# Attention with value products in four query quarters, and six key tiles' exponentials summed on GpSimd

## What is computed

```python
def layer(x):
    h = layernorm(x, eps=1e-6)
    q, k, v = split_heads(h @ w_qkv + b_qkv)              # 12 heads, 1024 x 32 each
    attn = (q * scale) @ k.T + rel_h + rel_w              # 1024 x 1024 per head, position terms from q
    x = x + (softmax(attn) @ v).merge_heads() @ w_proj + b_proj
    t = layernorm(x, eps=1e-5)
    # eight groups of 128 tokens, 8 experts, top 2, at most 40 tokens of a group per expert
    x = x + combine(relu(dispatch(t) @ wi[e]) @ wo[e])
    return x
```

## Time and profile before

| | before |
|---|---|
| median of 3 runs | 675.04 us |
| span of the profiled execution, first to last instruction | 670.8 us |
| of the run outside that span (675.04 less 670.8) | 4.2 us |
| PE busy in the span | 639.2 us, 95% |
| DVE, ACT, POOL busy | 391.9, 302.1, 29.4 us |
| share of the chain that ended last on PE | 90% |
| attention, from the first matmul of head 0 to the end of the last values | 81.91 to 333.04 us |

### The profile page before, as it was taken

One profiled execution on the slowest core, in us unless ns is written; L12 is line 12 of the kernel. 1 busy time (PEld: TensorE's weight loads), 2 busy tenths in 40 slices (PEclk: granted clock), 3 DMA queues, 4 the chain that ended last, 5 costly groups with the idle time before them and its releaser, 6 DMA issues.

```text
span 670.8 us, 10479 instructions
## 1 busy us (share of the span) xinstructions
PE 639.2 (95%) x3801; PEld 490.9 (73%) x3801; DVE 391.9 (58%) x664; ACT 302.1 (45%) x419; POOL 29.4 (4%) x49
## 2 busy tenths in 40 slices
PE   2999999999999999999986799999999999999996
PEld 2876845444444455544485699999999999999995
DVE  7557556545654556553176988555755566556735
ACT  4554234443444434444445453445444554444523
POOL 2300000000000000000030000000000000000000
PEclk9999999999999999999996799999999999999999
DMA  8045053331233213310115053445244434444302
GB/s 253 2 86 112 9 111 78 79 71 28 60 78 78 59 27 72 78 35 1 59 37 177 0 179 109 140 155 171 97 142 142 150 131 141 141 141 142 107 0 95
DMA packets 37406, 63.28 MB, mean 94 GB/s; under 512 B 3864, under 2 KB 32894, under 8 KB 37246
## 3 DMA queue, kind: packets, MB, share of 16 engines
q1 hardware_dynamic: 37374, 62.83, 33.6%
HBM read 44.16 MB, written 1.57 MB: 68 GB/s over the span
## 4 chain that ended last, share of the span: by engine, by line
PE 90%; DVE 4%; ACT 3%; DMA 1%; issue 1%; SPq 1%; DVEq 0%
PE ps L692 19%; PE ps L708 19%; PE ps L548 14%; PE ps L538 14%; PE ps L524 8%; PE ps L448 7%; PE ps L663 1%; PE ps L478 1%; PE ps L718 1%; DMA onehot<-c_onehot 1%; DVE rhalf L1034 1%; PE ps L642 1%; PE ps L725 1%; PE ps L555 1%; PE ps L726 1%
## 5 line engine op out<-in xcount | busy, mean ns | idle before, releaser
L1034 DVE TENSOR_REDUCE rhalf<-ps 128x1 f32<-128x512 f32 x192 | 126.7, 687 | 91.1 <-PE ps L524 87.8
L841 ACT ACTIVATE prob<-ps 128x1024 f32<-128x1024 f32 x96 | 98.2, 1023 | 154.6 <-PE ps L538 154.6
L538 PE MATMUL ps<-qst,kst 128*128 128x512 f32 x384 | 107.3, 401 | 0.0
L548 PE MATMUL ps<-prob,vh 128*64 128x512 f32 x384 | 103.6, 618 | 0.1
L692 PE MATMUL ps<-xeh,wih 128*128 128x320 f32 (+1 forms) x288 | 89.7, 312 | 1.0 <-ACT xeh L889 1.0
L538 PEld LDWEIGHTS ps<-qst,kst 128*128 128x128 f32 x384 | 69.9, 188 | 27.9 <-issue 14.6
L708 PE MATMUL ps<-hh,woh 128*128 128x320 f32 x288 | 89.3, 310 | 0.0
L708 PE MATMUL ps<-hl,woh 128*128 128x320 f32 x288 | 89.0, 309 | 0.0
L692 PE MATMUL ps<-xel,wih 128*128 128x320 f32 (+1 forms) x288 | 89.0, 309 | 0.0
L692 PE MATMUL ps<-xeh,wil 128*128 128x320 f32 (+1 forms) x288 | 89.0, 309 | 0.0
L708 PE MATMUL ps<-hh,wol 128*128 128x320 f32 x288 | 89.0, 309 | 0.0
(11 more groups left out here) (153 smaller groups left out, 766.5 us busy)
## 6 DMA issues: line engine op xcount, KB each, us to landing
raw_i<-in_L_ffn_wi SPq DMA_DIRECT2D x32, 576.0 KB, 5.0
raw_o<-in_L_ffn_wo SPq DMA_DIRECT2D x32, 576.0 KB, 4.0
xs<-in_x SPq DMA_DIRECT2D x8, 384.0 KB, 4.6
qst<-qh SPq DMA_DIRECT2D x12, 256.0 KB, 3.1
qst<-relh SPq DMA_DIRECT2D x12, 256.0 KB, 3.9
qst<-relw SPq DMA_DIRECT2D x12, 256.0 KB, 4.5
kst<-kp SPq DMA_DIRECT2D x12, 256.0 KB, 5.2
qst<-ql SPq DMA_DIRECT2D x12, 128.0 KB, 3.1
```

Of the source, the lines that this page charges most:

```text
L538: last = mm(bank(2 * (t % 2) + half), kst[b][:, part, t * P:(t + 1) * P], qst[b][:, part, half * BANK:(half + 1) * BANK], start=part == 0, ...
L548: last = mm(bank(6)[2 * HD * half:2 * HD * (half + 1), :], vh[b][:, t, :], prob[:, t % 2, half * BANK:(half + 1) * BANK], start=t == 0, st ...
L841: run(prob[:, t % 2, :], ps[:, 2 * (t % 2) * BANK:2 * (t % 2 + 1) * BANK], ACT.Exp).then_inc(exp_done, 1)
L1034: ve.tensor_reduce(rhalf[:, p // 2, p % 2:p % 2 + 1], bank(4 + p % 2), AX_X, ALU.max).then_inc(max_red, 1)
```

## The change

The change rebuilds `head` around pairs of key tiles, and does these things:

- **Quarters.** `vh` has 32 columns, values only. The queries are in four quarters of 256, and each has its own 32 columns of the array: a key tile is four matmuls of 256 columns (L560 in the changed kernel), which write columns 0 to 255 of bank 6.
- **Sums.** `prob` has four slots. GpSimd adds the exponentials of key tiles 0 to 5 into `acc` with five additions of 128 x 1024 (`add_probs`). At the end of a head PE multiplies tiles 6, 7 and `acc` with ones, again in quarters, into columns 256 to 511 of bank 6.
- **Pairs.** A head has four steps, each with two key tiles' scores, and values of two key tiles at once, two steps behind the scores; so the last two pairs of a head stand in the next head. The 16 pieces of `max_scores` stand as 5, 5, 6 and 0 in the four steps, and `turn_max` in the fourth.
- **Waits.** An exponential waits until its slot is free: for the values of the pair before and for GpSimd's addition of the tile that was there. GpSimd's first addition of a head waits until the values of the head before are through. `normalise` stands in front of piece 10 instead of piece 6 on DVE.
- **Last head and projection.** Two of the three chunks of heads are turned inside the last head, in banks 4 and 5; the third is turned between projection matmuls, which are reordered (chunks 0 and 1 of token tiles 0 to 4, then chunk 2). `residual` waits for each bias addition of GpSimd instead of all eight. Memory is moved accordingly.

```diff
-    vh = [new("vh0", [P, NT, 2 * HD]), new("vh1", [P, NT, 2 * HD]), place("vh2", [P, NT, 2 * HD], F32, o4 + 4 * BANK)]
+    vh = [new(f"vh{b}", [P, NT, HD]) for b in range(3)]
...
+            def add_probs(h):
+
+                pool.wait_ge(exp_done, NT * h + 2)
+                wait(pool, pv_mm, PAIRS_T * h)
+                nc.gpsimd.tensor_tensor(acc[:, :], prob[:, 0, :], prob[:, 1, :], ALU.add).then_inc(sum_add, 1)
+                for t in range(2, ADDED):
+                    pool.wait_ge(exp_done, NT * h + t + 1)
+                    pool.wait_ge(sum_add, (ADDED - 1) * h + t - 1)
+                    nc.gpsimd.tensor_tensor(acc[:, :], acc[:, :], prob[:, t % SLOT, :], ALU.add).then_inc(sum_add, 1)
...
+            def quarters(cols, stationary, moving, start, stop):
+
+
+                for j in range(4):
+                    last = mm(bank(6)[HD * j:HD * (j + 1), cols], stationary, moving[:, j * Q4:(j + 1) * Q4],
+                              start=start, stop=stop, skip_group_check=True)
+                return last
+
+            def values(h, b, i):
+                pe.wait_ge(exp_done, NT * h + 2 * i + 2)
+                if i == 0:
                     pe.wait_ge(vh_ready, h + 1)
                     wait(pe, o_copied, h)
-                for half in range(2):
-                    last = mm(bank(6)[2 * HD * half:2 * HD * (half + 1), :], vh[b][:, t, :],
-                              prob[:, t % 2, half * BANK:(half + 1) * BANK], start=t == 0, stop=t == NT - 1)
+                for t in (2 * i, 2 * i + 1):
+                    last = quarters(slice(0, Q4), vh[b][:, t, :], prob[:, t % SLOT, :], t == 0, t == NT - 1)
+                if i == PAIRS_T - 1:
+                    for t in range(ADDED, NT):
+                        quarters(slice(Q4, 2 * Q4), ones[:, 0:HD], prob[:, t % SLOT, :], False, False)
+                    pe.wait_ge(sum_add, (ADDED - 1) * (h + 1))
+                    last = quarters(slice(Q4, 2 * Q4), ones[:, 0:HD], acc[:, :], False, True)
                 last.then_inc(pv_mm, 1)
...
-            PIECES = [(0, 3), (3, 6), (6, 9), (9, 12), (12, 15), (15, 16), (16, 16), (16, 16)]
+            PIECES = [(0, 5), (5, 10), (10, 16), (16, 16)]
...
+                for i in range(PAIRS_T):
+                    pieces = [] if last else list(range(*PIECES[i]))
+                    if i > 1:
+                        values(h, b, i - 2)
+                    elif not first:
+                        values(h - 1, (b - 1) % 3, i + 2)
+                    if i == 2 and not first:
                         wait(pe, mneg_ready, h + 1)
                         turn_output(h - 1)
-                    for p in pieces[:1]:
-                        max_scores(h + 1, *nxt, p)
-                    if t == 1 and first:
+                    if i == 3 and not last:
+                        turn_max(h + 1)
+                    maxima(pieces[0:1])
+                    scores(h, b, 2 * i, 0)
+                    scores(h, b, 2 * i, 1)
+                    maxima(pieces[1:2])
+                    if i == 0 and first:
                         pe.wait_ge(v_dve, NT)
+                    scores(h, b, 2 * i + 1, 0)
+                    maxima(pieces[2:3])
+                    scores(h, b, 2 * i + 1, 1)
+                    maxima(pieces[3:])
...
+            def free_slot(h, t):
+
+
+                if t % 2 == 0:
+                    wait(act, pv_mm, PAIRS_T * h + t // 2 - 1)
+                if t < 2:
+                    wait(act, sum_add, (ADDED - 1) * h + t - 1)
+                elif t >= SLOT:
+                    wait(act, sum_add, (ADDED - 1) * h + max(1, t - SLOT))
```

More of the change, by code:

```diff
@@ L352, in _ @@
             nc.gpsimd.memset(ones[:, :], 1.0).then_inc(ones_set, 1)
-            for b in range(2):
-                nc.gpsimd.memset(vh[b][:, :, HD:2 * HD], 1.0).then_inc(ones_set, 1)
             pool.wait_ge(wqk_in, 16)
@@ L530, in turn_max @@
                 nc.tensor.transpose(bank(7)[0:NT, 0:P], rmax[:, :], ident[:, :]).then_inc(max_turned, 1)
[L532 to L535, removed]
-                for half in range(2):
-                    for part in range(2):
-                        last = mm(bank(2 * (t % 2) + half), kst[b][:, part, t * P:(t + 1) * P],
-                                  qst[b][:, part, half * BANK:(half + 1) * BANK], start=part == 0, stop=part == 1)
-                last.then_inc(s_mm, 1)
@@ L542, in values, with scores @@
-            def values(h, b, t):
-                pe.wait_ge(exp_done, 8 * h + t + 1)
-                if t == 0:
+            def scores(h, b, t, half):
+                if half == 0:
+                    if t == 0:
+                        pe.wait_ge(mrow_in, 16 * (h + 1))
+                    wait(pe, exp_done, NT * h + t - 1)
+                for part in range(2):
+                    last = mm(bank(2 * (t % 2) + half), kst[b][:, part, t * P:(t + 1) * P],
+                              qst[b][:, part, half * BANK:(half + 1) * BANK], start=part == 0, stop=part == 1)
+                if half == 1:
+                    last.then_inc(s_mm, 1)
@@ L556, in turn_output, with turn_attn @@
                 last.then_inc(o_turned, 1)
-            PIECES = [(0, 3), (3, 6), (6, 9), (9, 12), (12, 15), (15, 16), (16, 16), (16, 16)]
+            def turn_attn(c):
+                wait(pe, turn_dve, 2 * DC + 2 * c)
+                for half in range(2):
+                    for t in range(HALF):
+                        last = nc.tensor.transpose(bank(4 + half)[:, t * P:(t + 1) * P],
+                                                   attn[:, half * HALF + t, c * P:(c + 1) * P], ident[:, :])
+                    last.then_inc(turned, 1)
@@ L560, in head, with maxima @@
+            PIECES = [(0, 5), (5, 10), (10, 16), (16, 16)]
             def head(h, n, b, first=False, last=False):
                 nxt = (n + b // 2, (b + 1) % 3)
-                for t in range(NT):
-                    pieces = [] if last else list(range(*PIECES[t]))
-                    if t == 6 and not last:
-                        turn_max(h + 1)
-                    if t == 2 and not first:
+                def maxima(pieces):
+                    for p in pieces:
+                        max_scores(h + 1, *nxt, p)
+                for i in range(PAIRS_T):
[5 more added lines that the diff above has]
+                    if i == 2 and not first:
@@ L1058, in head @@
                 for p in range(2 * NT):
-                    if p == 6 and not first:
+                    if p == 10 and not first:
                         normalise(h - 1)
```

157 lines of the change are left out of this document (93 added, 64 removed).

## The result

| | before | after |
|---|---|---|
| median | 675.06 us (674.83 to 675.12, 4 runs) | 648.6 us (647.42 to 650.25, 4 runs) |
| span of the profiled execution | 670.8 us | 645.6 us |
| attention, from the first matmul of head 0 | 251.1 us | 228.5 us |

The ratio is 0.9616, with a 95% interval from 0.9598 to 0.9634. The forecast was 647.7.

The account below looks back on a forecast made before the run. PE, busy for 95% of the span, was taken to bound the kernel. From 675.04 us, 26.0 less in attention and 1.3 less behind it gave 647.7 us, with 640 to 656 as the range for 8 in 10.

Parts of the forecast that it names:

- Values in quarters: PE's value blocks in a head: 1.01 us per pair block, 2.32 for the last, 17.68 of PE work a head.
- The rival that four quarters don't run four abreast: PE's value blocks: if each group costs a quarter more, 14 us in all, giving 662 us; chance 0.07.
- The forecast's 3.54 a head: PE's work in a steady head: 17.68 us, 3.54 less than now, before any waits.
- The maxima are what is late next: Steady head: PE's maxima matmuls wait for DVE's reductions, 1.35 us a head, making the period 19.0.
- The walk: Step-by-step timing of maxima matmuls in a head: waits of 0.26, 0.26, then 0.31 and 0.42; the turning some 0.1.
- The spare time of 5.7: Steady heads: GpSimd's five additions, 2.5 us each, are hidden with 5.7 us to spare.
- Beyond, PE stands at `acc`: Steady heads: if GpSimd's additions take over 3.6 us each, PE waits at the `acc` product, delaying every engine.
- that rival: GpSimd's additions bound every head: slower than before from 4.0 us an addition, 703 us at 4.5; chance 0.04.
- First and last head: Ends of attention: head 0 takes 15.4 us; the last 19.7, or 1.35 longer if `wpl` locks GpSimd out.
- Behind attention: From the last value to the first residual addition: 7.5 us instead of 8.8, so 1.3 less.
- The clock rival: Behind attention: PE's granted clock falls before the small matmuls, 2.4 to 4 us come back, giving 651; chance 0.15.
- The same 4.2 around it: Outside the profiled span: median stays 4.2 us above the span, which was forecast at 643.5 us.

Follow-up runs that it names:

- experiment 6: The changed kernel with the old halves (32 columns of values, 32 of ones) and no GpSimd additions, pairs kept: 673.20 us, ratio 0.9976.
- experiment 5: The changed kernel without GpSimd's additions, PE multiplying all eight key tiles with ones in quarters: 673.01 us, ratio 0.9965.
- Experiments 1: The changed kernel with the maxima's matmuls spread, one behind each half of a key tile's scores: 638.76 us, ratio 0.9485.
- 2: The changed kernel with each maximum reduction over 128 of its 512 columns, leaving out three quarters of the scores: 632.37 us, ratio 0.9387.
- 10: The changed kernel with maxima's matmuls spread, `wpl` made early, and the output turned before step 3's block of values: 637.39 us, ratio 0.9448.
- experiment 3: The changed kernel with DVE's subtraction for `wpl` moved ahead of the heads' low part: 648.52 us, ratio 0.9616.

## Why the prediction was right, and where its terms were off

Forecast and measured time differ by 0.9 us. The mechanism held, but so small a difference is luck: attention took 3.4 more than forecast, and the stretch behind it and what lies around the span 1.6 and 1.2 less. By its steps:

- **Values in quarters: right.** A pair block took 1.00 (forecast 1.01), the last of a head 2.29 (2.32), PE's work in a head 17.66 (17.68). The rival that four quarters don't run four abreast is out. The Trainium skill, TensorE: Matmul & The Clock Gate, Part 3, has a ratio of 2.38 for three column tiles. This kernel's float32 products don't show it: two groups of four products of 256 columns took 1.00, and two abreast (experiment 6) took 1.87 for twice the columns.
- **What is saved comes from GpSimd: shown.** The forecast's 3.54 a head is the product with ones for six tiles, and seams and starts. Without the additions, with quarters (experiment 5) or halves (6), the kernel is within 0.4% of before. Quarters are only the form that lets the product with ones be left out.
- **The maxima are what is late next: right, and a cost was missing.** Experiments 1, 2 and 10 show it from three sides. The term of 1.35 a head measured 1.58. The walk had its waits nearly right: 0.26 and 0.26 in the first two steps, as measured, and 0.31 and 0.42 in the third, where the starts (208.16 and 209.33 above, and 208.65 between them) give 0.26 and 0.45. What it put at nothing is the 0.10 that a matmul which waited costs behind its start, three times a head; a row of the kernel before, the 0.50 instead of 0.40 of the matmul at 84.22, had it. "Two follow each other at 0.60" was too short as well, since the earlier trace rows gives (1.97 - 0.69) / 2 = 0.64 and here it is 0.67, but the first reduction behind the division started 0.2 sooner than the walk had it (2.40 of the step, for 2.6), so this cost nothing. Ten heads make 2.4 us of period (19.24 for 19.0).
- **GpSimd: right while it is hidden.** An addition took 2.40 for the 2.5 assumed, near the 2.57 in proportion to the 0.96 of 384 columns, and GpSimd idled 6.5 us a head before its first addition. The spare time of 5.7 was 6.1, and 0.73 pass from PE's start on `acc` to the next addition, for 0.8. "Beyond, PE stands at `acc`" is not what nine additions did: a slot was late first. The sum of that rival has a slip: by its own formula 4.5 us an addition gives 675 + 26 = 701, and not 703.
- **First and last head.** Head 0 took 15.58 (15.4). The last took 20.5 (19.7), and the difference is the one that the prediction told apart from its sum: the 0.93 that `wpl` held an addition (experiment 3). Without it the head would have been 19.6. The Trainium skill, SBUF — State Buffer, section SBUF: two separate sides, has this lock between GpSimd and a DVE operation with two SBUF inputs; the trace agrees, with 0.93 beside a `wpl` of 1.41, less than the 1.35 that the prediction estimated by it.
- **Behind attention: right to 0.1, and then a gain that wasn't forecast.** From the last value to the first residual 7.57 passed (7.5). The clock rival went the other way: the second small group took 3.57 instead of 5.26 before, so from the first residual to the experts it took 1.6 less. The granted clock was 0.50 in 332 to 334 and 0.96 beside the group. In the trace of experiment 3, with attention 1.0 shorter, that gain was gone. So the clock does move this stretch by 1.5 to 2 us; which way it falls, nothing in the trace of before could tell, and whether it falls the same way in every execution of a kernel stays open.
- **What lies around the span: wrong.** "The same 4.2 around it" set a median against the span of an execution that was shorter than the median. Executions of the kernel before that took 673.03 and 673.08 had a span of 670.8, so some 2.3 lie outside a span, and the other 1.9 is how much shorter the traced execution was than the median of 675.04. After, the median is 3.0 above the profiled span: 1.8 lie outside the span of that run (647.42), and 1.2 is what it stays under the median. The span was forecast 643.5 and measured 645.6: attention 3.4 longer, the stretch behind it 1.6 shorter, 0.3 in small pieces. So the span came 2.1 too short, and what lies around it 1.2 too long.

## What to carry to other kernels

When the bound engine gets work taken away, walk the next engine's operations in order against the new places of its inputs, and add to each wait what a waiting instruction costs behind its start. Here 1.6 of 3.5 us a head went into waits behind a two-bank ring, and spreading the producers over the same work won 9 to 10 us that the change had left (0.9616 to 0.9485). A period that comes out as forecast doesn't prove the link that was forecast: with nine additions the head took 23.9 for 23.3, and another wait made it. A saving of one microsecond is less than what executions of one kernel differ by here; before crediting it, or explaining its absence, read the stretch behind it, in more than one trace.

## What the runs showed of the hardware

- A GpSimd addition of 128 x 1024 float32 takes 2.40 us beside a DVE that reads PSUM, and 0.93 more when DVE works from two SBUF inputs beside it.
- The same 24 matmuls of 8 columns took 2.82, 3.57, 3.82, 4.48 or 5.26 us in these runs, by when the granted clock changed between 1.00 and 0.50; kernels that differ by 1 us ahead of it landed on either side. What decides it stays open: it wasn't tried by an experiment of its own, and each of these figures is from one execution.
- A reduction of 128 x 512 from PSUM takes 0.69 and of 128 x 128 0.29. The long ones follow each other 0.67 apart in rows, and 0.74 pass from the start of one to the matmul that it frees.
- A matmul of 512 columns that had to wait took 0.10 more up to the start of the next than one that hadn't (0.44 for 0.33 ahead of values, 0.34 for 0.23 ahead of scores).
